# Gathers issued ahead of the running maximum in halves of a round, and one layer's parts placed three key blocks later

## The reference, cut to what matters

```
cand = jnp.where(mask[..., None], h[:, None, :, :], NEG)   # layer 1
mx = cand.max(axis=2)
```

## Time and profile before

| | us |
|---|---|
| median of 3 runs | 9130.13 (9124.97 to 9143.81) |
| profiled execution, its own time | 9111.52 |
| its span | 9109.8 |
| PE busy | 5148.5 |
| DVE busy | 5894.4 |
| ACT busy | 4402.1 |
| POOL busy | 5128.1 |

### The profile page before, as it was taken

The page is one execution under the profiler, slowest core; times in us unless marked ns, Lnnn a source line. Parts: engine busy times, 40 slices in busy tenths (PEclk is TensorE's granted clock), DMA queues, the critical chain, the costliest instruction groups (busy, mean ns, idle before and its releaser), DMA issues.

```text
span 9109.8 us, 178961 instructions
## 1 busy us (share of the span) xinstructions
PE 5148.5 (57%) x60584; PEld 4779.8 (52%) x60584; DVE 5894.4 (65%) x7002; ACT 4402.1 (48%) x3608; POOL 5128.1 (56%) x5234
## 2 busy tenths in 40 slices
PE   3673750365765668365865667556845667362026
PEld 3672750364755557363865567555745567361025
DVE  5874860386867788486867687687847688581024
ACT  5644730165635566165735566356715566160034
POOL 0004777377764677377764677276764677377630
PEclk9885875687877878687987888788877888686568
DMA  2114332234332533135322433234322433132210
GB/s 99 43 34 124 66 66 25 46 69 113 61 63 65 122 65 80 19 76 133 67 62 66 119 66 83 58 75 101 69 48 66 120 65 80 54 55 58 23 26 29
DMA packets 307180, 629.05 MB, mean 69 GB/s; under 512 B 113553, under 2 KB 165906, under 8 KB 270610
## 3 DMA queue, kind: packets, MB, share of 16 engines
q0 software_dynamic: 91936, 161.87, 16.9%
q1 hardware_dynamic: 212354, 456.38, 14.2%
q10 hardware_dynamic: 2160, 0.06, 0.0%
HBM read 506.89 MB, written 111.15 MB: 68 GB/s over the span
## 4 chain that ended last, share of the span: by engine, by line
POOL 20%; issue 16%; DVE 14%; PE 13%; DMA 8%; ACT 4%; POOLq 2%; DVEq 2%; ACTq 1%; SPq 0%
DMA G<-table,idx 6%; POOL G L552 6%; POOL best L552 5%; PE ps L1413 4%; POOL best L538 4%; PE ps L1386 3%; PE ps L1415 2%; POOL best L535 2%; DVE keys L1077 2%; POOL G L535 2%; ACT Pbuf L689 1%; PE ps L1438 1%; DVE key L1067 1%; POOL best L537 1%; ACT Hn L689 1%
## 5 line engine op out<-in xcount | busy, mean ns | idle before, releaser
L552 POOL DMA_INDIRECT G<-table,idx x1416 | 1502.7, 1061 | 508.5 <-issue 452.7
L1415 PE MATMUL ps<-Hn,AT 128*128 128x99 bf16 x12288 | 1774.5, 216 | 0.0
L1415 PE MATMUL ps<-X,AT 128*128 128x99 bf16 x12288 | 1735.0, 214 | 52.6 <-issue 52.6
L544 POOL DMA_DIRECT2D idx<-lists x433 | 259.3, 599 | 2445.9 <-issue 1964.9
L689 ACT ACTIVATE Hn<-Rb,q 128x2048 int8<-128x2048 f32 x768 | 1485.4, 1988 | 86.6 <-PE ps L1415 82.1
L689 ACT ACTIVATE Pbuf<-Rb,q 128x2048 int8<-128x2048 f32 x768 | 1487.8, 1987 | 18.2 <-PE ps L1415 15.6
L552 POOL DMA_INDIRECT best<-table,idx x1024 | 1093.7, 1068 | 319.4 <-issue 309.3
L1415 PEld LDWEIGHTS ps<-X,AT 128*128 128x128 fp8e4 x12288 | 1243.2, 101 | 57.6 <-issue 57.6
L1415 PEld LDWEIGHTS ps<-Hn,AT 128*128 128x128 fp8e4 x12288 | 1256.5, 102 | 0.0
L1413 PE MATMUL ps<-X,Hn 128*128 128x198 bf16 x6144 | 933.6, 268 | 567.6 <-DVE Hn L937 358.6
L1413 PE MATMUL ps<-Hn 128*128 128x198 bf16 x6144 | 960.3, 272 | 433.0 <-DVE Zs L957 236.0
(11 more groups left out here) (186 smaller groups left out, 11171.7 us busy)
## 6 DMA issues: line engine op xcount, KB each, us to landing
Rb<-in_adj SPq DMA_DIRECT2D x128, 1024.0 KB, 6.3
Rb<-rrows SPq DMA_DIRECT2D x104, 1024.0 KB, 6.3
bytes_A<-A SPq DMA_DIRECT2D x128, 256.0 KB
bytes_AT<-AT SPq DMA_DIRECT2D x128, 256.0 KB
AT<-bytes_AT SPq DMA_DIRECT2D x128, 256.0 KB, 3.6
AT<-bytes_A SPq DMA_DIRECT2D x128, 256.0 KB, 4.6
G<-table,idx POOLq DMA_INDIRECT x1416
h<-Hn SPq DMA_DIRECT2D x16, 1024.0 KB, 4.1
```

The lines of the kernel that those rows point to most:

```text
L544: pool.dma_start(idx[:, slot, :], lists[bass.ds(r, 1)].rearrange("o p k -> (o p) k")).then_inc(idx_in[slot], 16)
L552: pool.indirect_dma_start(out=dst[:, k, :], out_offset=None, in_=table, in_offset=bass.IndirectOffsetOnAxis(ap=idx[:, slot, k:k + 1], axis ...
L1415: ins = pe.matmul(both[:, 0, 0:G], A8[:, jb, at], v[:, 0:G], start=False, stop=jb == T - 1, skip_group_check=True)
```

## The change

POOL: `G` is now the running maximum and has four rows, `best` receives all gathers, eight rows in two halves. A half's gathers of the next round are issued as soon as that half of `best` has been merged (the first half of a tile's first round is copied to G instead). The list arrives in one slot of `idx` and is copied, half by half, into the other, from which the gathers read. A list is fetched two rounds ahead of the round just merged, across tiles and, at a graph's last tile, across graphs; there no gathers are issued ahead. Four gathers share one semaphore. The tree has two levels instead of three. SP writes one more list after the last one, which the fetch after the last round reads.

PE and DVE: the steps of the sage layer begin at key block 4 instead of 1 (`SAGE_AT`). DVE's sums begin at block 7 instead of 4, the last statistics come at block 15, and both parts of the deviations follow there, where they were at 12 and 13.

```
-            def rows_of(fetched, slot, dst):
+            def ask(v, r, part):
                 plain(pool)
-                pool.wait_ge(idx_in[slot], fetched * 16)
+                pool.wait_ge(idx_in, r * 16 + 16)
                 settle(pool)
-                for k in range(KEYS):
+                v(pool.tensor_copy(asked[:, half(part)], arrived_idx[:, half(part)]))
+                settle(pool)
+                for k in range(part * (KEYS // 2), (part + 1) * (KEYS // 2)):
                     pool.indirect_dma_start(
...
             def tile(b, t, last):
                 lo, hi = number(b, t), number(b, t + 1)
+                v = Chain(pool, merged, lo * MERGE, MERGE)
+                landed(lo, 0)
+                settle(pool)
+                v(pool.tensor_copy(G[:, :, :], best[:, half(0), :]))
+                if not last:
+                    ask(v, lo + 1, 0)
+                landed(lo, 1)
+                greater(v, G[:, :, :], best[:, half(1), :])
+                if not last:
+                    ask(v, lo + 1, 1)
+                    fetch(lo + 2)
...
                 with pool.Fori(lo + 1, hi) as r:
+                    w = Chain(pool, merged, r * MERGE, MERGE)
                     if last:
+                        for part in range(2):
+                            ask(w, r, part)
+                        fetch(r + 1)
+                    for part in range(2):
+                        landed(r, part)
+                        greater(w, G[:, :, :], best[:, half(part), :])
+                        if not last:
+                            ask(w, r + 1, part)
+                    if not last:
+                        fetch(r + 2)
...
             def gather(b):
+                v = Chain(pool, first_asked, b * 2, 2)
+                for part in range(2):
+                    ask(v, first, part)
+                fetch(first + 1)
...
-                        between.append((p + 4, lambda p=p: sage_sums(other, p)))
-                        between.append((p + 5, lambda p=p: sage_statistics(other, p)))
-                    between.append((T // 2 + 4, lambda: rest_of.append(deviations(4, other))))
-                    between.append((T // 2 + 5, lambda: rest_of[0]()))
+                        between.append((p + SAGE_AT + 3, lambda p=p: sage_sums(other, p)))
+                        between.append((p + SAGE_AT + 4, lambda p=p: sage_statistics(other, p)))
+                    between.append((T - 1, lambda: rest_of.append(deviations(4, other))))
+                    between.append((T - 1, lambda: rest_of[0]()))
...
-                if jb == 1:
+                if jb == SAGE_AT:
                     sage_arrived(b)
```

More of the change, by code:

```diff
@@ L79, in build @@
     END_AT = 2
+    SAGE_AT = 4
     EXP_AT = 5
@@ L100, in build @@
         best = sb("best", [P, KEYS, F])
-        G = sb("G", [P, KEYS, F])
+        G = sb("G", [P, KEYS // 2, F])
         idx = sb("idx", [P, 2, KEYS], U32)
+        asked, arrived_idx = idx[:, 0, :], idx[:, 1, :]
         key = sb("key", [P, KW], F16)
@@ L247, in build @@
         list_in = sem("list_in")
-        idx_in = [sem("idx_in0"), sem("idx_in1")]
-        got = [sem(f"got{s}") for s in range(KEYS)]
+        idx_in = sem("idx_in")
+        got = [sem(f"got{s}") for s in range(2)]
         merged = sem("merged")
+        first_asked = sem("first_asked")
         tree = sem("tree")
@@ L470, in middle @@
             def middle(b, alone):
+                if alone:
+                    total = sp.value_load(cum[0:1, bass.ds(B * (T + 1) - 1, 1)], min_val=0, max_val=ROUNDS)
+                    plain(sp)
+                    sp.wait_ge(idx_ready, total)
+                    sp.wait_ge(list_in, total * 16 + 16)
+                    settle(sp)
+                    sp.dma_start(lists[bass.ds(total, 1)].rearrange("o p k -> (o p) k"), found_idx[:, :]).then_inc(list_in, 16)
                 with sp.Fori(0, T) as t:
@@ L572, in tile @@
+                if not last:
[5 more added lines that the diff above has]
+                    fetch(lo + 2)
+                settle(pool)
+                pool.sem_inc(merged, MERGE - v.n)
                 with pool.Fori(lo + 1, hi) as r:
+                    w = Chain(pool, merged, r * MERGE, MERGE)
                     if last:
-                        fetch(r, 1)
@@ L575, in tile @@
[L575 to L586, removed]
@@ L587, in tile @@
-                    v.end()
+                        for part in range(2):
[8 more added lines that the diff above has]
+                        fetch(r + 2)
+                    w.end()
@@ L588, in tile @@
                     settle(pool)
-                if not last:
-                    fetch(hi, 0)
                 v = Chain(pool, tree, (b * T + t) * TREE, TREE)
-                for width in (4, 2, 1):
-                    greater(v, best[:, 0:width, :], best[:, width:2 * width, :])
+                for width in (2, 1):
+                    greater(v, G[:, 0:width, :], G[:, width:2 * width, :])
                 settle(pool)
-                v(pool.tensor_copy(Agg[:, bass.ds(t, 1), :].rearrange("p o f -> p (o f)"), best[:, 0, :]))
+                v(pool.tensor_copy(Agg[:, bass.ds(t, 1), :].rearrange("p o f -> p (o f)"), G[:, 0, :]))
@@ L597, in tile @@
                 v.end()
-                if not last:
-                    plain(pool)
-                    pool.wait_ge(idx_in[1], hi * 16)
                 settle(pool)
@@ L609, in gather @@
                 settle(pool)
-                fetch(number(b, 0), 0)
+                first = number(b, 0)
+                if isinstance(b, int) and b == 0:
+                    fetch(first)
+                v = Chain(pool, first_asked, b * 2, 2)
+                for part in range(2):
+                    ask(v, first, part)
+                fetch(first + 1)
                 with pool.Fori(0, T - 1) as t:
@@ L1364, in sage_step @@
             def sage_step(b, jb):
-                if jb == 1:
+                if jb == SAGE_AT:
                     sage_arrived(b)
[L1368 to L1371, removed]
+                if 0 < jb - SAGE_AT <= T // 2:
+                    sage_product(b, jb - SAGE_AT - 1)
+                if 0 <= jb - SAGE_AT < T // 2:
+                    sage_turned(b, jb - SAGE_AT)
             def sums(L, hn, other):
@@ L1501, in beside @@
                 if b is None:
-                    for jb in range(T // 2 + 2):
+                    for jb in range(T):
                         sage_step(other, jb)
```

23 lines of the change are left out of this document (11 added, 12 removed).

## The result

The change made the kernel slower. Its runs have a median of 9254.74 us (9245.70 to 9263.21, four runs), beside 9127.55 for the kernel before (9104.63 to 9143.81, four runs): a ratio of 1.014, 95% interval 1.0118 to 1.0161. That is +127 us where I had forecast +60. The profiled execution took 9245.7 us against 9111.5 before, +134; its span is 9244.0 against 9109.8.

What follows compares the result with a forecast made beforehand. POOL's gather was taken to bound seven graphs of eight. POOL's +64 us counted as +56, plus +2 for sage: +58 on the profiled 9111.5, 9169.5; medians run 18.6 higher, so 9188, rounded to 9190, range 9000 to 9300.

Steps and rivals of the forecast that it cites:

- The case I forecast: Whole kernel: slower, 9150 to 9260 us, POOL's added list copies and bursts outweighing the waits removed; chance 0.47.
- DMA waits removed: POOL's waits for landing gathers ahead of the fetch and of a first maximum all disappear: -290 us.
- Fetches: POOL's list fetches fall from 433 to 306, with preparation hidden behind gathers and shorter loop and tile starts: -442 us.
- copy into G: POOL, 128 new copies of 512 columns, 0.746 us each plus 0.08 of lead: +106 us.
- Copies of the list: POOL, 610 awaited copies of 128x4 numbers, two per round, at 1.05 us per ask: +640 us, ends +220 and +1000.
- (b): The list copy's own time on POOL: between 0.10 and 0.42 us, taken as 0.20.
- (a): Gap ahead of each list copy on POOL, wait and settle: 0.26 us.
- (c): Gap between a list copy and its first gather on POOL: between 0.30 and 1.26 us, taken as 0.86.
- The new wait for a list: POOL waits in the 177 further rounds for a fetch queued behind four gathers: +50 us, between nothing and 290.
- rival of the late list: The fetch behind four gathers lands late in each further round, 225 us there: +150 over the forecast, 9330 us; chance 0.11.
- Sage part: Later sage steps: joins 1.6 us earlier in six graphs (-10), graph 4 +12, last graph 0; sum +2 us.
- the factor 7/8: Graph 4 has other bounds, so only 7/8 of POOL's +64 us counts: +56 us.

Runs made afterwards that it cites:

- whole rounds: Changed kernel with one eight-column list copy and one burst of eight gathers per round: 9096.35 us, ratio 0.992; with sage steps back at block 1, 9039.64 us, 0.9891.
- the sage steps alone: Kernel before with only the sage layer's steps moved from key block 1 to 4, POOL as it was: 9155.12 us, ratio 1.0017.
- the gathers alone: Changed kernel with the sage steps back at key block 1: 9222.77 us, ratio 1.0089.
- best version: Kernel before with the tree's first level moved right behind issuing the first further round's gathers: 9027.06 us, ratio 0.9847; again 9007.40 us, 0.9851.
- the kernel with no copies: Changed kernel without list copies, each list half fetched into its own place once that half's gathers landed: 9376.78 us, ratio 1.023.

## Why the prediction was right in direction and short in size

The case I forecast came true: an ask costs more than it hides. The sum for POOL was +64 and measured +154. Of the 154 us, 118 lie in the seven graphs where PE waited before. Of the 36 in graph 4, 23 arrived, as its join came 929.6 us behind the table's landing instead of 906.6. The other joins gave back 12, and 5 came at the two ends: +134 between the traces. By kind of POOL instruction, each with the idle time ahead of it, in the eight gathers (forecast from the terms on record, measured from the two traces):

| kind | forecast | measured | off |
|---|---|---|---|
| fetches with the waits ahead of them (-204, -128, -213, and 128 x 2.49 of tile starts) | -864 | -899 | -35 |
| copies into G (with 128 x 1.99 of tile starts) | +361 | +348 | -13 |
| gap ahead of gathers (610 x 0.56, less 46) | +296 | +277 | -19 |
| the gathers' own time | +18 | +67 | +49 |
| list copies, own time | +122 | +222 | +100 |
| list copies, gap ahead | +159 | +131 | -28 |
| list copies, waiting for the list | +50 | +148 | +98 |
| maxima, copies to Agg, waits ahead | -77 | -140 | -63 |
| sum | +65 | +154 | +89 |

Point by point:

- *DMA waits removed, -290:* right. 0.6 us of landing waits remain ahead of the maxima. The maxima and copies to Agg themselves ran 53 us shorter, which no term had; without that piece of luck the miss would be larger.
- *Fetches, -442, and copy into G, +106:* right to 40 us together.
- *Copies of the list:* the step that failed is (b), "I take 0.20, as four columns are near the first". The copy takes 0.364 on average. I had judged it by its width and put the work of VectorE beside it at nothing. Line, engine and count, then the shortest, median and longest in ns:

```profile
L565 POOL COPY idx<-idx x610: 182/187/4266, 751.3 to 8867.3; 128x4 uint32<-128x4 uint32 x153
```

  So the 0.20 is right for the median. In the trace, 356 of the 610 copies overlap no two-input instruction of VectorE (TENSOR_TENSOR, SCALAR_TENSOR_TENSOR): they take 0.185 on average and never more than 0.254. The 254 that overlap one take 0.616. That excess, 109 us, is the whole +100. (a) was 0.20 to 0.27 rather than 0.26, (c) 0.79 rather than 0.86, with 25 leads of 3.42 that bring the mean to 0.90.
- *The new wait for a list:* the second step that failed. "Four gathers queue less than eight or sixteen: +50" was an argument without a row. It is 148 us in 54 waits, most of them (34 waits, 114 us, counted over 0.8 us) behind a maximum and 24 us behind the short copy into G. The DMA issues of the kernel after (count, size, median us to landing) show a later landing, against 1.9 us in rows 8 (from the 128 fetches whose landing that trace has, 120 of them issued ahead of a tree with no gather in front):

```profile
idx<-lists POOLq DMA_DIRECT2D x306, 4.0 KB, 3.5
```

  My rival of the late list had 225 in the further rounds, so the truth lies between the two. With the fetch issued ahead of the second burst the wait was gone. That move takes four gathers from in front of the fetch, and it also gives the list more time, 11.8 us in the median from the fetch to the copy that reads it against 7.3. With whole rounds the fetch stands behind eight gathers and lands after 4.2 us in the median, and with 11.4 us to the copy only 4.9 us are waited. So the gathers in front delay the list, and the short time to its use makes the delay a wait; how much of the 148 us each makes was not separated. In the traces with the same order of fetches it is 148, 165 (sage steps early) and 123 us (copies doubled).
- *Sage part, +2:* its terms were right (joins 56.8 to 58.9 behind the maxima, graph 4 +9 when alone), and one was missing. In the medians it costs 18 us alone (interval 1 to 31), 42 on top of the gathers and 32 on top of whole rounds, the last two between runs that did not stand beside each other. What the traces show of it runs through POOL.
- *Graph 4, the factor 7/8:* I had written that POOL would have to be 25 us slower in that graph to matter. It was 36 slower (872.3 against 836.2 us), and PE waits 9.56 us there. So 23 us arrived from graph 4, where the forecast had 12. This follows from the mis-sized terms, not from a wrong mechanism.

**How the sage steps reach POOL.** A timeline of the kernel after, POOL and DVE, late in graph 5's gathers, where the last blocks of LB sums that now stand ahead of PE's wait run beside POOL:

```profile
6795.18 0.19 POOL L565 COPY idx<-idx 128x4 uint32<-128x4 uint32 x1 [0.26 <-POOL G L584]
6795.38 4.61 DVE L927 SCALAR_TENSOR_TENSOR Pbuf<-Rb,q,AT 128x2048 f32<-128x2048 f32 x2 [0.38 <-DVE found_idx L1101]
6796.16 2.45 POOL L568 DMA_INDIRECT best<-table,idx  x1 [0.80 <-POOL idx L565]
...
6803.34 1.27 POOL L546 TENSOR_TENSOR best<-best,G 128x512 f32<-128x512 f32 x1
6803.72 3.05 DVE L927 SCALAR_TENSOR_TENSOR Pbuf<-Rb,q,AT 128x2048 f32<-128x2048 f32 x1 [3.73 <-PE ps L1405]
6804.81 2.43 POOL L548 TENSOR_SCALAR best<-best 128x512 f32<-128x512 f32 x1 [0.20 <-POOL best L546]
6807.29 3.44 DVE L927 SCALAR_TENSOR_TENSOR Pbuf<-Rb,q,AT 128x2048 f32<-128x2048 f32 x1 [0.53 <-PE ps L1405]
6807.32 1.26 POOL L549 TENSOR_TENSOR G<-G,best 128x512 f32<-128x512 f32 x1
6808.78 2.00 POOL L565 COPY idx<-idx 128x4 uint32<-128x4 uint32 x1 [0.20 <-POOL G L549]
```

Both engines stretch. The clamp at 6804.81 takes 2.43 us where it takes 0.61 undisturbed, and ends 0.47 us behind the weighing (6803.72 + 3.05 = 6806.77). The list copy at 6808.78 takes 2.00 instead of 0.19, and ends at 6810.78, 0.05 behind the weighing of 6807.29. The gather's issue at 6796.16 takes 2.45 instead of 0.94. VectorE in turn takes 3.05 and 3.44 us where the same instruction beside no POOL work takes 2.35:

```profile
2739.43 2.35 DVE L927 SCALAR_TENSOR_TENSOR Pbuf<-Rb,q,AT 128x2048 f32<-128x2048 f32 x1 [56.58 <-PE ps L1405]
```

The Trainium skill (SBUF — State Buffer, Who interferes with whom) states that a VectorE instruction with two inputs in SBUF contends with a GpSimd instruction that reads SBUF, since its second input comes through a read interface that the two share, and that issue order decides who blocks. The weighing reads two tensors, and this trace agrees for POOL: the list copy, the clamp and the gather's issue, which start well inside a weighing, end 0.05, 0.47 and 0.9 us behind its end, each within its own undisturbed length. It does not settle the order. The weighing of 6807.29 starts 0.03 us ahead of POOL's maximum, and is the one that grows, by 1.09 us, while the maximum takes its usual 1.26.

Added up from the traces, POOL's instructions beside a weighing took longer than the median of the same instruction elsewhere: by 45 us in the kernel before (52 us of overlap), 68 with the sage steps alone (93), 54 with the gathers alone (71) and 80 with both (110); for whole rounds 76 (91) with the steps late and 42 (52) with them early. So each time that the steps move to block 4, some 40 us more of weighing lie beside POOL, and POOL loses 22 to 34 us by it. The gathers grew by 33, 36 and 55 us in these three pairs of traces. The best version's gathers differed by 36 us between two traces of the same kernel, so what else is in these growths is not shown.

**What stays open.** Why a lead of 3.42 us comes once in 96 gathers in the changed kernel, and not with whole rounds. Why gathers land later in some rounds, and in some traces of the same kernel, than in others, and so how much of the 154 to 186 us left in the best version can be had. The best version was not combined with the change's fetching two rounds ahead.

## What to carry to other kernels

Hiding a latency by splitting a burst costs one awaited lead per piece: here 1.2 us for each of 610 asks (0.2 ahead, 0.36 copy, 0.6 more lead behind), against 290 us of waits to win. Count the pieces before the waits. Work that has to be done anyway, put between the issue and the wait, hid half the waits for 45 us. Price a new instruction with its neighbours: the small copy takes 0.19 us in the median and 0.364 on average, by what another engine does beside it. And when work of another engine is moved under a wait, ask what it does to the engine that everybody is waiting for.

## What was not expected of the hardware

- A copy of 128x4 numbers on POOL takes 0.185 us beside no two-input instruction of VectorE, 0.616 on average beside one, and up to 4.27.
- A fetch of 4 KB behind four gathers lands after 3.5 us in the median and behind eight after 4.2, against 1.9 with mostly none in front; behind four its reader waited in 54 cases, up to 5.7 us.
- The first gather behind an awaited instruction has a lead of 0.79 us behind a copy, and 0.83 behind a maximum in the kernel with no copies (273.1 us in 330 cases); behind a fetch it has 0.30. A fetch behind an awaited copy has 0.86.
- One lead in 96 gathers is 3.42 us, in the changed kernel, with the sage steps early or late, and with the copies doubled. With the fetch behind the copy, leads of 1.57 to 2.11 us come at the same distance.
